# Twenty-four down products of a mixture-of-experts kernel computed as three fp32r products each, with the activation's lower part taken by VectorE or GpSimd

## The reference

```
x: (8, 256, 128)   ctx: (8, 256, 96)
q = layernorm(x) @ Wq.T ; k = ctx @ Wk.T ; v = ctx @ Wv.T
sim = q k^T, made zero mean and unit variance over each whole 256x256 batch
x  = x + (softmax(sim) @ v) @ Wo.T
h  = layernorm(x)
p  = softmax(h @ gate_w + gate_b); the two largest of 8 kept as cw, others 0
out = x + shared(h) + sum_e cw[e] * expert_e(h)
expert(h): a, b = split(h @ w1 + b1); (silu(a) * b) @ w2 + b2      (FF = 128)
```

## Time and profile before

| | us |
|---|---|
| median of 3 runs | 138.81 (138.77 to 139.99) |
| the profiled execution, its own time | 139.75 |
| its span | 137.7 |
| PE busy | 128.4 (93%) |
| DVE busy | 103.5 (75%) |
| ACT busy | 71.1 (52%) |
| POOL busy | 22.7 (16%) |

### The profile page before, as it was taken

The page is one execution under the profiler, slowest core; times in us unless marked ns, Lnnn a source line. Parts: engine busy times, 40 slices in busy tenths (PEclk is TensorE's granted clock), DMA queues, the critical chain, the costliest instruction groups (busy, mean ns, idle before and its releaser), DMA issues.

```text
span 137.7 us, 2007 instructions
## 1 busy us (share of the span) xinstructions
PE 128.4 (93%) x603; PEld 92.8 (67%) x603; DVE 103.5 (75%) x308; ACT 71.1 (52%) x135; POOL 22.7 (16%) x40
## 2 busy tenths in 40 slices
PE   0999799998999999999999999999999999999992
PEld 0777578766777655877777765787657766666662
DVE  1549777777999998946987999629997882875672
ACT  2534968897432139991642249952332884313140
POOL 7081403226280001140400020000400000000000
PEclk9999999999999999999999999999999999999999
DMA  4999400000930000039300002059100014910022
GB/s 126 288 306 258 146 0 7 0 0 14 317 133 0 5 0 0 2 72 380 162 5 0 0 0 76 5 187 381 48 0 0 23 58 132 401 79 0 5 76 76
DMA packets 8828, 12.97 MB, mean 94 GB/s; under 512 B 1321, under 2 KB 6994, under 8 KB 8306
## 3 DMA queue, kind: packets, MB, share of 16 engines
q1 hardware_dynamic: 8242, 12.62, 27.2%
q10 hardware_dynamic: 576, 0.23, 0.7%
HBM read 11.73 MB, written 1.11 MB: 93 GB/s over the span
## 4 chain that ended last, share of the span: by engine, by line
PE 49%; issue 31%; POOL 8%; DVE 5%; ACT 2%; DMA 2%; POOLq 0%; DVEq 0%
PE bank L907 43%; POOL row_powers L367 3%; POOL w_rest L391 3%; DMA ctx_sb<-in_ctx_dram 2%; POOL ln_rstd L376 2%; PE bank L969 1%; PE bank L923 1%; POOL sim_r L382 1%; PE bank L999 1%; PE bank L1022 1%; DVE x L818 1%; PE bank L1082 1%; DVE g_beats L760 1%; PE bank L915 1%; DVE g_rank L763 1%
## 5 line engine op out<-in xcount | busy, mean ns | idle before, releaser
L527 ACT ACTIVATE silu<-bank,b_cols 128x512 f32<-128x512 f32 (+1 forms) x37 | 25.0, 677 | 39.7 <-PE bank L907 39.2
L907 PE MATMUL bank<-x_head,w_head 128*128 128x512 f32 x72 | 38.8, 538 | 0.0
L907 PE MATMUL bank<-act,w_sb 128*128 128x512 f32 x68 | 34.7, 592 | 0.0
L797 DVE TENSOR_TENSOR silu<-silu,cw_all 128x512 f32<-128x512 f32 (+1 forms) x31 | 20.7, 669 | 12.2 <-DMA cw_all<-cw_dram 8.4
L805 DVE SCALAR_TENSOR_TENSOR act<-bank,b_cols,silu 128x512 f32<-128x512 f32 (+1 forms) x37 | 27.2, 736 | 3.0 <-ACT silu L527 1.7
L907 PE MATMUL bank<-x_head,w_rest 128*128 128x512 f32 x72 | 28.5, 395 | 0.0
L907 PE MATMUL bank<-x_rest,w_head 128*128 128x512 f32 x72 | 28.3, 393 | 0.0
L907 PEld LDWEIGHTS bank<-x_head,w_head 128*128 128x128 f32 x72 | 13.6, 189 | 7.1 <-issue 3.1
L907 PEld LDWEIGHTS bank<-x_rest,w_head 128*128 128x128 f32 x72 | 13.6, 190 | 6.3 <-issue 5.0
L907 PEld LDWEIGHTS bank<-x_head,w_rest 128*128 128x128 f32 x72 | 13.5, 188 | 3.2
L907 PEld LDWEIGHTS bank<-act,w_sb 128*128 128x128 f32 x68 | 12.6, 189 | 2.6
(11 more groups left out here) (118 smaller groups left out, 175.9 us busy)
## 6 DMA issues: line engine op xcount, KB each, us to landing
cw_all<-cw_dram SPq DMA_DIRECT2D x4, 1024.0 KB, 6.9
cw_all<-cw_dram SPq DMA_DIRECT2D x4, 512.0 KB, 4.9
cw_all<-cw_dram SPq DMA_DIRECT2D x6, 256.0 KB, 3.6
x_sb<-in_x_dram SPq DMA_DIRECT2D x4, 256.0 KB, 4.1
w_sb<-in_L_ffn_rw_dram SPq DMA_DIRECT2D x1, 1024.0 KB, 7.7
ctx_sb<-in_ctx_dram SPq DMA_DIRECT2D x4, 192.0 KB, 4.1
out_dram<-x SPq DMA_DIRECT2D x3, 256.0 KB, 2.1
w_sb<-in_L_ffn_rw_dram SPq DMA_DIRECT2D x1, 512.0 KB, 6.4
```

The costliest lines, as they stand in the source:

```text
L527: scalar.activation(silu[:, k, cols], hid(n, 0)[:, cols], ACT.Silu, bias=b1_cols[:, 0, e:e + 1]).then_inc(silu_sb, 1)
L797: dve.tensor_tensor(silu[:, k, cols], silu[:, k, cols], cw_all[:, e - 1, cols], ALU.mult).then_inc(scaled_sb, 1)
L907: return pe.matmul(dst, lhs, rhs, start=start, stop=stop, skip_group_check=True)
```

## The change

1. The down products of slots 9 to 32 (24 of them) are divided as the hidden ones are: `w2_head`·`act_head`, `w2_rest`·`act_head`, `w2_head`·`act_rest`. The other down products stay as they were.
2. ACT copies `act` to `act_head` (`act_heads(n-2)` behind the silu of slot n). `act_rest = act - act_head` is made by DVE in place 1 of slot n for n-2 = 10, 11, 16, 19, 20, 25 and 27 to 32, and by POOL for the other twelve, between its places 0 and 1.
3. `down(n-3)` stands at the end of slot n, and `act` has four buffers. In the last slot `down(32)` and `down(33)` stand between the two hidden products.
4. `w2_head` and `w2_rest` are made once, in three groups of three experts, by ACT (slots 4 to 6) and POOL (slots 5 to 7).
5. The normalisation of chunks two to four goes from DVE to ACT (`normalise`, slots 3, 12, 21, behind the input, u and v copies); DVE keeps one small instruction, `second_shift`.
6. The opening: six PE products of constants that nobody reads stand first; the statistics of the first chunk come after `center_qk`, those of the second after `scores_scale(0)`; POOL makes `scores_rstd(0)` ahead of `first_rstd(1)`; the loads of wo and wv have a semaphore each. On POOL `first_rstd` and `scores_rstd` move one slot later or behind the rests. `out_bias` moves from e = 2 to e = 3.

```diff
+        UNREAD = 6
+        DIVIDED = list(range(NX, LAST - STRAIGHT))
+        W2_GROUPS = [(0, 3), (3, 6), (6, NX)]
+        DOWN_BEHIND = 3
+        BY_VECTOR = [n for n in DIVIDED if n >= NX * (C - 1) or n % NX in (1, 2, 7)]
+        BY_POOL = [n for n in DIVIDED if n not in BY_VECTOR]
-        POOL_AT = {'first_rstd': [-9, 1], 'scores_rstd': [-2, 0], 'second_rstd': [4, 0]}
+        POOL_AT = {'first_rstd': [-8, 1], 'scores_rstd': [-1, 1], 'second_rstd': [4, 0]}
@@ POOL
+            def act_rests(n):
+                pool.wait_ge(act_head_sb, divided(n))
+                pool.tensor_tensor(act_rest[:, n % 3, :], act[:, n % 4, :], act_head[:, n % 3, :].bitcast(F32), ALU.subtract).then_inc(pool_rest_sb, 1)
...
                 for piece, c in due(POOL_AT, n, 0):
                     pieces[piece](c)
+                if 5 <= n < 5 + len(W2_GROUPS):
+                    w2_rests(n - 5)
+                if n - 2 in BY_POOL:
+                    act_rests(n - 2)
@@ ACT
+            def normalise(c, g):
+                scalar.wait_ge(shift_sb, upto(c, g))
+                scalar.wait_ge(x2t_ps, done(c - 1))
+                for i in batch_tiles(groups(c)[g]):
+                    last = scalar.activation(xn[:, i, :], x1[:, TC * c + i, :], ACT.Identity, bias=ln_shift[:, i:i + 1], scale=ln_rstd[:, i:i + 1])
+                last.then_inc(xn_ready, 1)
+            def act_heads(n):
+                scalar.wait_ge(act_sb, n + 1)
+                scalar.wait_ge(y_ps, n - 2)
+                copy(act_head[:, n % 3, :], act[:, n % 4, :]).then_inc(act_head_sb, 1)
...
                 if n >= 1:
                     expert_silu(c, e)
+                if n - 2 in DIVIDED:
+                    act_heads(n - 2)
@@ DVE
-                    if n >= 3:
-                        dve.wait_ge(y_ps, n - 2)
+                    if n >= 4:
+                        dve.wait_ge(y_ps, n - 3)
+                    if n - 4 in BY_POOL:
+                        dve.wait_ge(pool_rest_sb, BY_POOL.index(n - 4) + 1)
...
-                expert_gate(c, e, lambda: run(n, 1))
+                def between():
+                    if n - 2 in BY_VECTOR:
+                        act_rests(n - 2)
+                    run(n, 1)
+
+                expert_gate(c, e, between)
@@ PE
-                pe.wait_ge(act_sb, n + 1)
-                mm(OUT_B[:, :], w2_sb[:, e, :], act[:, k, :], e == 0, n in (NX * (c + 1) - 1, LAST - STRAIGHT)).then_inc(y_ps, 1)
+                first, final = e == 0, n in (NX * (c + 1) - 1, LAST - STRAIGHT)
+                if n in DIVIDED:
+                    pe.wait_ge(w2_rest_sb, len(W2_GROUPS))
+                    if n in BY_POOL:
+                        pe.wait_ge(pool_rest_sb, BY_POOL.index(n) + 1)
+                    else:
+                        pe.wait_ge(dve_rest_sb, BY_VECTOR.index(n) + 1)
+                    mm(OUT_B[:, :], w2_head[:, e, :], act_head[:, k, :], first, False)
+                    mm(OUT_B[:, :], w2_rest[:, e, :], act_head[:, k, :], False, False)
+                    mm(OUT_B[:, :], w2_head[:, e, :], act_rest[:, k, :], False, final).then_inc(y_ps, 1)
+                else:
+                    pe.wait_ge(act_sb, n + 1)
+                    mm(OUT_B[:, :], w2_sb[:, e, :], act[:, n % 4, :], first, final).then_inc(y_ps, 1)
...
+            ones = nc.const_aps.tensor_like(1.0, ident[:, :])
+            for _ in range(UNREAD):
+                mm(LATE[:, 0:P], ones, ones)
```

More of the change, by code:

```diff
@@ L135, in xattn_moe_kernel @@
         silu = sb("silu", [P, 3, N])
-        act = sb("act", [P, 3, N])
+        act = sb("act", [P, 4, N])
+        act_head, act_rest = sb("act_head", [P, 3, N], F32R), sb("act_rest", [P, 3, N], F32R)
         out_t = sb("out_t", [P, N])
@@ L414, in _ @@
             first_rstd(0)
+            scores_rstd(0)
             first_rstd(1)
-            scores_rstd(0)
             pool.wait_ge(w1_rest_sb[1], 1)
@@ L519, in w1_heads, with w2_heads @@
                 copy(head, whole).then_inc(w1_head_sb[g], 1)
+            def w2_heads(g):
+                lo, hi = W2_GROUPS[g]
+                scalar.wait_ge(w2_in, 32)
+                copy(w2_head[:, lo:hi, :], w2_sb[:, lo:hi, :]).then_inc(w2_head_sb, 1)
+            def act_heads(n):
+                scalar.wait_ge(act_sb, n + 1)
+                scalar.wait_ge(y_ps, n - 2)
+                copy(act_head[:, n % 3, :], act[:, n % 4, :]).then_inc(act_head_sb, 1)
             def expert_silu(c, e):
@@ L539, in _ @@
                 scalar.dma_start(dst[:, :], src).then_inc(qk_in, 16)
-            for dst, src in ((wo_sb, wo), (wv_sb, wv)):
-                scalar.dma_start(dst[:, :], src).then_inc(vo_in, 16)
+            scalar.dma_start(wo_sb[:, :], wo).then_inc(wo_in, 16)
+            scalar.dma_start(wv_sb[:, :], wv).then_inc(wv_in, 16)
             ctx_copy(0)
@@ L650, in second_shift @@
                 dve.wait_ge(ln_r[1], upto(c, g))
+                if c >= 1:
+                    dve.wait_ge(xn_ready, done(c - 1))
                 dve.scalar_tensor_tensor(ln_shift[:, t], ln_mv[:, 1, t, 0], -1.0, ln_rstd[:, t], ALU.mult, ALU.mult).then_inc(shift_sb, 1)
-            def second_normalise(c, g):
-                dve.wait_ge(ln_r[1], upto(c, g))
-                if c >= 1:
-                    dve.wait_ge(x2t_ps, done(c - 1))
-                for i in batch_tiles(groups(c)[g]):
-                    last = dve.tensor_scalar(xn[:, i, :], x1[:, TC * c + i, :], ln_mv[:, 1, i, 0:1],
-                                             ln_rstd[:, i:i + 1], ALU.subtract, ALU.mult)
-                last.then_inc(xn_ready, 1)
             def scores_statistics(m):
@@ L802, in expert_gate, with act_rests @@
                     dve.wait_ge(b_ps, n + 1)
-                    if n >= 3:
-                        dve.wait_ge(y_ps, n - 2)
-                    dve.scalar_tensor_tensor(act[:, k, cols], hid(n, 1)[:, cols], b1_cols[:, 1, e:e + 1], silu[:, k, cols],
+                    if n >= 4:
+                        dve.wait_ge(y_ps, n - 3)
+                    if n - 4 in BY_POOL:
+                        dve.wait_ge(pool_rest_sb, BY_POOL.index(n - 4) + 1)
+                    dve.scalar_tensor_tensor(act[:, n % 4, cols], hid(n, 1)[:, cols], b1_cols[:, 1, e:e + 1], silu[:, k, cols],
                                              ALU.add, ALU.mult).then_inc(act_sb, 1)
+            def act_rests(n):
+                dve.wait_ge(act_head_sb, divided(n))
+                dve.tensor_tensor(act_rest[:, n % 3, :], act[:, n % 4, :], act_head[:, n % 3, :].bitcast(F32), ALU.subtract).then_inc(dve_rest_sb, 1)
             def final(c):
@@ L1093, in straight_down @@
                         tile = slice(i * P, (i + 1) * P)
-                        last = mm(TILE_BANKS[i][:, 0:D], act[:, n % 3, tile], w2_sb[:, n % NX, :], False, n == LAST)
+                        last = mm(TILE_BANKS[i][:, 0:D], act[:, n % 4, tile], w2_sb[:, n % NX, :], False, n == LAST)
                         if n == LAST:
@@ L1164, in _ @@
                 if n == LAST:
+                    down(n - 3)
                     down(n - 2)
@@ L1176, in _ @@
                 run(n, 3)
-                if 2 <= n < LAST:
-                    down(n - 2)
+                if DOWN_BEHIND <= n < LAST:
+                    down(n - DOWN_BEHIND)
                 if e == 1 and by_product(c, e):
```

33 lines of the change are left out of this document (21 added, 12 removed).

## The result

The changed kernel takes 146.41 us (median of 4 runs, 144.56 to 147.12) against 139.39 for the kernel before on the same chip (138.77 to 139.99): a ratio of 1.046, 95% interval [1.034, 1.058]. It is slower, as forecast, but by 7.0 us where the forecast had 2.9, and above the range, whose end was 145.5.

The account below looks back on a forecast made before the run. PE was taken as paced by its own work in most slots, with DVE, ACT and a DMA right behind. The terms -1.0 - 1.0 + 0.5 + 3.5 - 0.9 + 1.75 = +2.85 on 138.81 gave 141.7 us, range 135.0 to 145.5.

Parts of the forecast that it names:

- slots 16 to 21: ACT's copies delay the cw rows; PE waits for POOL's rests at down(15) and down(18): +3.5, bounds +1.5 and +5.
- slots 22 to 26: Five divided down products with cover save PE time: -0.9, bounds -0.9 and +1.
- opening and slots 0 to 8: Opening, earlier clock rise less DVE's later statistics: -1.0; chunk one, normalisation taken off DVE: -1.0.
- slots 9 to 15: PE waits for POOL's rest of n = 9, DVE has more work, PE's saving gives some back: +0.5, bounds -0.7 and +1.8.
- slots 27 to 35 and the end: Copies delay chunk four's cw rows, then DVE needs 2.1 a slot against PE's 2.07: +1.75, bounds 0 and +2.5.
- The -1.0 for the normalisation in chunk one: Slots 0 to 8: taking the normalisation off DVE, where it waited for POOL's subtraction: -1.0, between -2.3 and 0.
- The wait of 0.7 at down(9): Slots 9 to 15: POOL's root stands ahead of the rest of n = 9, so PE waits 0.7.
- rival three: DVE's two-input instructions wait for POOL's rests at the shared port, slots 11 to 19: +4.2, 145.9 us; chance 0.17.
- Rival one: PE keeps its pace, ACT's copies fit its gaps: faster, 134.0 us, up to 137.4 with one wait left; chance 0.25.
- two: Gains and waits cancel, the wait at down(18) is absorbed later: no change, 138.8 +- 1.4 us; chance 0.17.

Follow-up runs that it names:

- work in the wait: Changed kernel with twelve unread fp32r products on PE ahead of down(18), where it waits: 145.00 us, ratio 1.041 to the kernel before.
- root behind the rest: Changed kernel with POOL's second layernorm reciprocal root placed behind the rest of the same slot: 143.03 us, ratio 1.027 to the kernel before.
- nothing divided: Changed kernel with all down products plain f32, act neither copied nor subtracted, everything else kept: 139.23 us, ratio 0.999 to the kernel before.
- no rests: Changed kernel without its 24 subtractions; the third product reads act_head once more, copies stay: 139.43 us, ratio 1.002 to the kernel before.
- copies unread: Changed kernel with no down product divided, but ACT's 24 copies of act kept unread: 140.77 us, ratio 1.011 to the kernel before.
- unread subtractions, placed: Kernel before with the change's opening, POOL's pieces in the change's places and twelve unread POOL subtractions: 139.94 us, ratio 1.004 to the kernel before.
- unread writes: Kernel before with the change's opening, POOL's pieces in the change's places and twelve POOL memsets that read nothing: 138.84 us, ratio 0.996.

## Why the forecast was right in sign and wrong in size

Two steps failed: in slots 16 to 21 the sum set a delay worked out on the old clock behind gains that it already contained (1.5 us short), and in slots 22 to 26 the fall of PE's clock behind the computed wait was put at nothing (about 1.8 us in the four runs at 0.988, 2.5 in the profiled one). Set against the forecast's own terms, by the table of slots:

| term | forecast | profile | off by |
|---|---|---|---|
| opening and slots 0 to 8 | -2.0 | -2.15 | -0.15 |
| slots 9 to 15 | +0.5 | +1.24 | +0.7 |
| slots 16 to 21 | +3.5 | +5.06 | +1.6 |
| slots 22 to 26 | -0.9 | +1.23 | +2.1 |
| slots 27 to 35 and the end | +1.75 | +2.25 | +0.5 |
| sum | +2.85 | +7.6 | +4.8 |

**The opening and chunk one.** The sum is right by luck, its parts are not. The opening gives -1.5 by the runs (forecast -1.0, within its bounds), but I had made the -1.0 of -1.9 for the clock and about +1.0 for VectorE's later statistics: the unread products alone give -0.8, and the new order costs nothing (-0.4, and 0.7 of the whole opening's -1.5 beyond the unread products). The -1.0 for the normalisation in chunk one came as -0.75 in slots 3 to 8 and was gone at slot 9: the earlier trace rows do show VectorE standing 1.3 us for POOL, but chunk one ends with the router's chain, which the normalisation was not in front of, and there PE waits 0.91. In the profile a lucky opening (-2.2) hid the miss.

**Slots 9 to 15.** The wait of 0.7 at down(9) that I had worked out did not come. The whole loss stands in slot 15 (slot 15 is still 2.16 ahead, slot 16 is 0.91), in the wait of 1.19 for VectorE's router rows. The shift of slot 12, 1.05 longer beside POOL's rest (65.69 above), costs PE nothing; the moments of slot 14, 1.09 longer (74.79), are rows of the engine that PE then waits for. Without rests slot 15 loses 0.2, with the unread subtractions in POOL's places alone 0.6, and with all rests on VectorE 0.65: so about half of it is rival three's mechanism; how the other half comes about is not shown.

**Slots 16 to 21.** This step failed, but less in its mechanism than in its arithmetic. The mechanism of its second half came within 0.7 us at each point: PE waits at down(18), put down to POOL's rest; the root begins at 97.51 (98.2 in the working), the rest ends at 100.1 (100.6), slot 22 begins at 101.69 (101.3). In its first half PE waits 0.76 at down(15), not 1.9. But that 101.3 is a point on the clock of the kernel before, and so holds everything that went ahead of it, while the sum added it as +3.5 to the -1.5 of the slots ahead. The sum therefore put slot 22 at 97.75 + 2.0 = 99.75, 1.5 us ahead of its own working. Of its inner steps one was wrong: the cw rows were to be 1.2 later and are 0.11 later (87.50 against 87.39 in the earlier trace rows). They are late only against the opening's gain, which should have brought them up to two microseconds earlier. That gain was gone by slot 18, and the port can take most of it: with nothing but the unread subtractions PE waits 1.20 for the same row of VectorE ahead of 85.54 (1.32 in the changed kernel), and loses 1.7 us from slot 9 to slot 18, against 2.2.

**Slots 22 to 26.** The second failed step, and a missing term. "Five down products with cover" gave -0.9; the profile has +1.2. After a wait of 2.89 us PE ran at its lower clock up to slot 23. I had read from the earlier trace rows that PE starts at that level, had worked out a wait of over 2 us, and did not ask whether such a wait would bring the level back. With work in the wait the clock stayed at 1.00, and the same five slots gave -0.8, 2.0 better. But only there, where PE came to slot 22 late and everything lay ready for it: with the root behind the rest, also at 1.00, PE comes 3.7 us earlier and the five slots give +0.4. So most of what the term lacked was the clock, and the cover it counted on is there only for a PE that is late. At 1.00 the changed kernel takes 144.5 us, which is inside the range, but still 2.3 us more above the kernel before than was forecast (5.1 against 2.85).

**Slots 27 to 35.** The size was nearly right, the place only in part. From 122.96 on VectorE has hardly a gap (two, of 0.33 and 0.51), as forecast, and PE's wait at down(32) came as forecast (0.68, for VectorE's rest). The most is lost behind slot 35, +1.6, where down(32) and down(33) stand ahead of the last hidden product (with nothing divided that place costs 0.9); but nearly as much, +1.24, is lost in slot 27, by the table loads and the rest behind them, which the working did not have. Between the two, slots 28 to 34 gave back 0.6.

**The rivals.** Rival one (PE keeps its pace) and two are out. Rival three was true in its mechanism, and its 4.2 us is about the sum of the excess lengths (1.05, 1.09, 0.98, 0.41 and 0.85 in the five longest rows of the last three chunks; the fourth is line 840 of slot 19 at 92.77, where 0.75 was forecast, the fifth that of slot 28). As a price it was two to three and a half times too high: with the same twelve subtractions in the same places, and the down products left whole, the end came 2.1 us later, 1.2 of it by the reading. That its number, 145.9, came near to the 146.4 is chance.

**Where the 6.1 us of the rests go.** The profiles of the runs above, each counted from slot 9 so that its opening doesn't matter, lose against the kernel before:

| kernel | slots 9 to 15 | 16 to 21 | 22 to 26 | 27 to the end | in all |
|---|---|---|---|---|---|
| changed | +1.2 | +5.1 | +1.2 | +2.25 | +9.8 |
| root behind the rest | +1.2 | +1.3 | +0.4 | +2.25 | +5.2 |
| no rests | +0.1 | -0.1 | +1.1 | +0.2 | +1.3 |
| copies unread | +0.5 | 0.0 | +1.05 | +1.1 | +2.7 |
| nothing divided | 0.0 | -0.25 | +0.3 | +0.9 | +0.9 |
| unread subtractions, placed | +0.6 | +1.1 | +0.4 | 0.0 | +2.2 |
| unread writes | 0.0 | +0.1 | +0.8 | 0.0 | +0.8 |

2.6 us are the root's order with the lower clock that follows from it. The remaining 3.5 by the runs (3.8 here) are the second row less the third: 1.1 in slot 15, 1.4 in slots 16 to 21, most of it in slot 17, and 2.1 from slot 27 on (1.1 in slot 27, 0.9 behind slot 35), while 0.7 is given back in slots 22 to 26. In the first two of these places the unread subtractions alone lose 0.6 and 1.1. The copies' 1.8 and the divided products' -1.3 all but cancel.

**What stays open.** These are single profiles, good to some tenths. What makes the part of slot 15's loss that the port alone does not make (0.5 of 1.1) is not shown, nor is the half us by which the kernel with the filled wait is slower than the changed one at the same clock.

## What to carry to other kernels

A step worked out on the clock of the old trace already holds whatever came ahead of it: add it to earlier gains only if its chain moves with them. When a product is divided, its new inputs inherit every queue that they pass: a product that needed `act` alone now waits for a rest behind a table load on ACT, behind a root in POOL's written order, and behind VectorE's hold on POOL. And a wait of PE of some 3 us should be priced with the slower products behind it; filling it, or better moving one entry of one order so that it does not arise, is worth more than the 0.18 us a product that was being sought.

## What the runs showed of the hardware

A POOL memset left VectorE's small two-input rows alone (0.17 and 0.16 above), but not these one-input ones: beside the memset of 1.16 us that began at 97.30 the four normalisations take 1.74 us, against 1.12 alone and 2.08 beside a subtraction in the same place (98.05 in the run with the unread subtractions).

```profile
97.38 1.74 DVE L663 TENSOR_SCALAR xn<-x,ln_mv,ln_rstd 128x128 f32<-128x128 f32 x4
```

And the hold goes both ways: POOL's rest lasts 1.26 to 1.30 when it begins alone and 1.69 when a two-input row of VectorE had begun just ahead of it (110.97 and 111.09 above; 117.76 and 117.89 in the changed kernel).
